# Where the sync queue requests the output weights and the input of tiles 3 to 8 in an attention and mixture-of-experts layer

## The chip, the cores and the metric

The kernel runs on one core of a Trainium2 chip, in one launch. The metric is the device time of an execution in microseconds, and less is better. All times of the trace are counted from the start of the span, which is the time from the first to the last instruction that the profiler recorded.

## The reference, cut to what matters

Two batches of 1024 tokens with 256 features go through two halves of a layer, all in float32. The change touches only the first half, and of that only when its data are fetched.

```
x = x + attention(layernorm(x), ctx)          # 16 heads of 16, 77 keys per batch
    q = layernorm(x) @ w_q.T
    k, v = ctx @ w_k.T, ctx @ w_v.T
    out = softmax(q k^T / 4) v  @ w_o.T
x = x + ffn(layernorm(x))
    shared = silu(x @ sw1.T) * (x @ sw3.T) @ sw2.T
    routed: each token goes to its best 2 of 8 experts, each of the same form as shared
```

## The kernel before, in words

The 2048 tokens are 16 tiles of 128 tokens. The program has one block, with a hand-written list of instructions for each engine (TensorE, VectorE, ScalarE, GpSimd, SyncE), and semaphores between them. Nothing reorders the lists: an instruction that waits holds up all that stand behind it on its engine. The DMA requests are part of these lists too, so a request that waits holds up the requests behind it on the same queue.

The attention half goes through the tiles with a loop over `i` (lines 1143 to 1170 on TensorE). In round `i` TensorE makes the scores of tile `i` (`scores`, lines 986 to 988 by way of `product`), multiplies the probabilities of tile `i - 1` with the values (`attended`, line 1056), transposes the row maxima (`peaks`, line 1031) and subtracts them (`shifted`, line 1039), makes the query of tile `i + 1` (`queries`, line 1010), transposes the probabilities (line 1045), and projects tile `i - 1` with the output weights `wo` (`projected`, line 1072). `queries` waits for its input once per group of tiles: tile 3 waits for `xt2_in`, which stands for the input of tiles 3 to 8 in `x_t`. `projected` waits once, at tile 0, for `wo_in`, and then for `at_out`, ScalarE's copy of the transposed attention (line 474).

Ahead of the loop stands the preparation. TensorE makes the raw keys (line 1130) and the column means of the query's weights (line 1136). VectorE subtracts the means (line 786, semaphore `centred`); TensorE then makes the first query with the centred weights `wq_c`, and after it the raw values (line 999). ScalarE copies the values out of PSUM (`hid`, line 474) and stores them to a scratch tensor `value_rows` in HBM (line 564, 154 KB in rows of 16 floats, semaphore `v_stored`). SyncE reads them back in another layout, with partitions that run over heads and keys (lines 311 and 313, semaphores `v_in0` and `v_in1`, tiles `v_rows` and `act_s`). VectorE spreads the values over three columns of heads (`values`, lines 624 and 626, tile `vals`), and this is what `attended` multiplies with.

The queue of SyncE stands in this order: five requests for the first tiles and the key weights, which wait for nothing (lines 300 to 304); the four reads of the values, which wait for `v_stored`; the input of tiles 3 to 8 (line 315, 768 KB); `wo` (line 316, 256 KB); the residual rows of tiles 3 to 7 (line 317, 640 KB); and then the feed-forward weights in 27 parts of 256 KB by way of four stage buffers `w_stage` (line 323), with the rest of the input (lines 320 and 321) between the fourth and the fifth. ScalarE's queue asks for the context, `wq`, `wv`, the gate and the bias at the start, and stores `value_rows` later. ScalarE and GpSimd split the feed-forward weights into a high and a low part beside the attention (lines 499 and 424), ScalarE from round 2 on.

Behind the attention, tokens are scattered into lists of their experts (GpSimd, line 415), read back by SyncE (line 340) and put through the experts' weights by TensorE (line 992 for the transposes, 986 to 988 for the products).

Of the kernel before, what the change touches and what calls it, by code (L numbers as in the profile page):

```python
# [124 lines left out]
def need(eng, semaphore, value):  # L125
    if value > 0:
        eng.wait_ge(semaphore, value)
# [14 lines left out]
def cols(n, width=DIM):  # L142
    return bass.ds(n * width, width)


def v3(t, a):
    return t.rearrange("p (a b) -> p a b", a=a)


def tiles_of(tokens):  # L150

    return [tokens[b * SEQ:(b + 1) * SEQ, :].rearrange("(p t) d -> p t d", p=P) for b in range(BATCH)]


def rows_of(tokens, t, n):

    u = t % TILES_PER_BATCH
    return tiles_of(tokens)[t // TILES_PER_BATCH][:, u:u + n, :]


def layer_kernel(nc, x, xt, ctxt, wqt, wkt, wvt, wot, gatet, bias, wffn, out):
    def sb(name, n, dt=F32):
        return nc.alloc_sbuf_tensor(name, [P, n], dt)
# [23 lines left out]
    wq_c, wo = (sb(n, KT * DIM) for n in ("wq_c", "wo"))  # L187
# [100 lines left out]


    links_of = [2 + 2 * n + 6 for _, n in GROUPS]  # L290
    links_before = [sum(links_of[:g]) for g in range(len(GROUPS))]

    with nc.Block() as block:

        @block.sync
        def _(sp):
            x_tiles = tiles_of(x)
            resid_tiles = v3(resid[:, :], TILES)
            xt_tiles, turned = xt.rearrange("p (t d) -> p t d", d=DIM), v3(x_t[:, :], TILES)
            sp.dma_start(wk, wkt).then_inc(s["wk_in"], 16)  # L300
            sp.dma_start(turned[:, 0:1, :], xt_tiles[:, 0:1, :]).then_inc(s["xt0_in"], 16)
            sp.dma_start(resid_tiles[:, 0:1, :], x_tiles[0][:, 0:1, :]).then_inc(s["x0_in"], 16)
            sp.dma_start(turned[:, 1:3, :], xt_tiles[:, 1:3, :]).then_inc(s["xt1_in"], 16)
            sp.dma_start(resid_tiles[:, 1:3, :], x_tiles[0][:, 1:3, :]).then_inc(s["x1_in"], 16)


            sp.wait_ge(s["v_stored"], 16)
            sp.wait_ge(s["filled"], 16)
            for b in range(BATCH):
                to = v3(v_rows[b], CHUNKS)  # L310
                sp.dma_start(to[:, 0:WHOLE_CHUNKS, :], value_rows[b, 0:WHOLE_CHUNKS * P, :]
                             .rearrange("(c p) d -> p c d", p=P)).then_inc(s[f"v_in{b}"], 16)
                sp.dma_start(to[0:CHUNK_REST, WHOLE_CHUNKS, :],
                             value_rows[b, WHOLE_CHUNKS * P:, :]).then_inc(s[f"v_in{b}"], 16)
            sp.dma_start(turned[:, 3:9, :], xt_tiles[:, 3:9, :]).then_inc(s["xt2_in"], 16)
            sp.dma_start(wo[:, :], wot).then_inc(s["wo_in"], 16)
            sp.dma_start(resid_tiles[:, 3:TILES_PER_BATCH, :], x_tiles[0][:, 3:, :]).then_inc(s["x2_in"], 16)
            for n, part in enumerate(PART_ORDER):
                if n == STAGES:
                    sp.dma_start(turned[:, 9:, :], xt_tiles[:, 9:, :]).then_inc(s["xt3_in"], 16)  # L320
                    sp.dma_start(resid_tiles[:, TILES_PER_BATCH:, :], x_tiles[1]).then_inc(s["x3_in"], 16)
                need(sp, s["split_lo"], (n - STAGES + 1) * (PART // PIECE))
                sp.dma_start(w_stage[:, cols(n % STAGES, PART)],
                             wffn[:, cols(part, PART)]).then_inc(w_in[n % STAGES], 16)

            sp.wait_ge(s["pads_done"], 4)
            sp.dma_start(lists[EXPERTS * REGION:, :], pad_rows[:, :]).then_inc(s["pad_out"], 16)
            sp.wait_ge(s["counted"], 1)
            _, n_rows = nc.values_load_multi_w_load_instructions(counts_i[0:1, :], engines=(mybir.EngineType.SP,))
            for e in range(EXPERTS):  # L330
                sp.dma_start(lists[bass.ds(n_rows[e] + e * REGION, P), :], pad_rows[:, :]).then_inc(s["pad_out"], 16)
            sp.wait_ge(s["table_step"], TABLE_LINKS)
            sp.wait_ge(s["pad_out"], 16 * (EXPERTS + 1))
            for n in range(ROW_BUFS):
                sp.wait_ge(scat[n], 16 * TOPK * (TILES // ROW_BUFS))
            for j in range(TILES_B):
                row = sp.value_load(row_i[j:j + 1, 0:1], min_val=0, max_val=EXPERTS * REGION)
                need(sp, s["b_t_ps"], j - LIST_BUFS + 1)
                need(sp, s["b_meta"], j - LIST_BUFS + 1)
                sp.dma_start(list_rows[:, cols(j % LIST_BUFS, ROW)],  # L340
                             lists[bass.ds(row, P), :]).then_inc(b_in[j % LIST_BUFS], 16)

            for par in range(2):
                sp.wait_ge(b_out[par], 16 * ((TILES_B + 1 - par) // 2))
            token_rows = results[0:RESULTS, :].rearrange("(t k) d -> t (k d)", k=TOPK)
            for n, (t, tiles) in enumerate(READS):
                sp.dma_start(sum_tiles[:, t:t + tiles, :], rows_of(token_rows, t, tiles)).then_inc(c_in[n], 16)
            for n, (t, tiles) in enumerate(SUM_GROUPS):
                sp.wait_ge(s["c_sum"], n + 1)
                sp.dma_start(rows_of(out, t, tiles), resid_tiles[:, t:t + tiles, :]).then_inc(s["c_out"], 16)  # L350
            sp.wait_ge(s["c_out"], 16 * len(READS))
# [965 lines left out]
```

## Time and profile before

| | us |
|---|---|
| median of 3 runs | 299.66 |
| lowest and highest | 298.84, 300.81 |
| the profiled execution's own time | 295.51 |
| its span | 293.7 |
| TensorE busy in the span | 278.0 (95%) |
| VectorE, ScalarE, GpSimd busy | 185.9, 165.6, 143.8 |

The profiled execution's time holds the span and 1.8 us around it. The trace is one execution, so waits and durations read from it belong to 295.51 us and not to the median.

### The profile page before, as it was taken

To read this page: it belongs to the slowest core of one execution; us is meant where nothing else is said; L and a number is where in the kernel's file an instruction comes from. 1 tells how busy PE (TensorE), PEld (TensorE's weight loads), DVE (VectorE), ACT (ScalarE), POOL (GpSimd) and SP (SyncE) were. 2 spreads that over 40 slices of the span, in tenths; PEclk is the share of its full clock that TensorE was granted. 3 is DMA by queue.
4 is the path that set the end of the run, shared out by engine and by line. 5 is a ranking of instruction groups with operands and counts; after the bars stand their busy time and mean duration, and the time that the engine had idled before them with its cause. 6 is when DMAs were issued, how large, how long until landed. Compare 5 with 4: busy or idle time off the path is not lost.

```text
span 293.7 us, 6561 instructions
## 1 busy us (share of the span) xinstructions
PE 278.0 (95%) x1989; PEld 244.7 (83%) x1989; DVE 185.9 (63%) x700; ACT 165.6 (56%) x404; POOL 143.8 (49%) x234
## 2 busy tenths in 40 slices
PE   7689999999999999999985999999999999999966
PEld 7478889988988999987764898888888998888855
DVE  1648555556765778776874466666766666653675
ACT  2147787778867655556432355665666555554421
POOL 8004776666698837765660013333333333333390
PEclk9999999999999999999998699999999999999999
DMA  7269633343341112211282213333333333211796
GB/s 234 26 158 405 224 102 105 107 108 95 95 138 56 37 39 74 75 55 59 73 234 63 72 54 112 108 98 106 111 110 107 98 107 111 90 44 49 261 390 226
DMA packets 23996, 35.37 MB, mean 120 GB/s; under 512 B 8123, under 2 KB 14907, under 8 KB 23835
## 3 DMA queue, kind: packets, MB, share of 16 engines
q1 hardware_dynamic: 17072, 24.43, 27.1%
q0 software_dynamic: 3408, 9.41, 9.1%
q10 hardware_dynamic: 3483, 1.11, 1.6%
q8 instruction: 18, 0.29, 0.4%
q14 instruction: 15, 0.12, 0.1%
HBM read 22.07 MB, written 12.87 MB: 119 GB/s over the span
## 4 chain that ended last, share of the span: by engine, by line
PE 86%; DMA 4%; DVE 3%; POOL 2%; issue 2%; ACT 1%; SPq 0%; DVEq 0%; POOLq 0%
PE psum L986 15%; PE psum L987 13%; PE psum L988 13%; PE psum L1056 13%; PE psum L992 9%; PE psum L1010 6%; PE psum L1045 5%; PE psum L1072 5%; POOL lists L415 2%; PE psum L1039 2%; DMA lists<-rows,dest 2%; PE psum L1090 1%; DMA value_rows<-hid 1%; PE psum L1125 1%; DMA v_rows<-value_rows 1%
## 5 line engine op out<-in xcount | busy, mean ns | idle before, releaser
L451 POOL DMA_INDIRECT results<-probs_t,place x39 | 37.2, 955 | 81.0 <-ACT probs_t L558 81.0
L1056 PEld LDWEIGHTS psum<-vals,probs_t 128*128 128x128 f32 x320 | 37.9, 192 | 3.2 <-issue 2.6
L1056 PE MATMUL psum<-vals,probs_t 128*128 128x51 f32 x320 | 39.9, 274 | 0.3 <-DVE vals L626 0.3
L424 POOL TENSOR_TENSOR w_lo<-w_stage,w_hi 128x256 fp32r<-128x256 f32 x54 | 37.8, 730 | 4.5 <-ACT w_hi L499 4.5
L415 POOL DMA_INDIRECT lists<-rows,dest x32 | 31.7, 990 | 16.5 <-DVE dest L761 9.3
L543 ACT ACTIVATE act_s<-psum,share 128x256 f32<-128x256 f32 x39 | 18.5, 475 | 32.3 <-PE psum L988 32.3
L986 PE MATMUL psum<-w_lo,x_hi 128*128 (+1 forms) x82 | 36.2, 441 | 0.0
L800 DVE TENSOR_REDUCE row_max<-psum 128x16 f32<-128x1232 f32 x16 | 23.0, 1438 | 20.5 <-PE psum L988 20.4
L854 DVE TENSOR_TENSOR h_lo<-psum,h_hi 128x256 fp32r<-128x256 f32 x55 | 23.3, 423 | 20.1 <-ACT h_hi L474 20.1
L986 PE MATMUL psum<-w_lo,h_hi 128*128 (+1 forms) x110 | 31.8, 289 | 3.3 <-DVE h_lo L854 3.3
L988 PE MATMUL psum<-w_hi,x_hi 128*128 (+1 forms) x82 | 32.4, 395 | 0.0
L987 PE MATMUL psum<-w_hi,x_lo 128*128 (+1 forms) x82 | 32.3, 394 | 0.0
L987 PE MATMUL psum<-w_hi,h_lo 128*128 (+1 forms) x110 | 31.4, 285 | 0.0
L988 PE MATMUL psum<-w_hi,h_hi 128*128 (+1 forms) x110 | 31.3, 284 | 0.0
L850 DVE SCALAR_TENSOR_TENSOR hid<-psum,share,act_s 128x256 f32<-128x256 f32 x39 | 18.9, 484 | 14.8 <-ACT act_s L543 14.8
L986 PEld LDWEIGHTS psum<-w_lo,h_hi 128*128 128x128 f32 x110 | 21.0, 191 | 7.6 <-DVE h_lo L854 4.6
L474 ACT ACTIVATE h_hi<-psum 128x256 fp32r<-128x256 f32 x55 | 20.8, 378 | 10.4 <-PE psum L992 10.4
L488 ACT ACTIVATE probs<-psum,rstd 128x616 f32<-128x616 f32 x32 | 23.0, 770 | 4.7 <-PE psum L1039 4.7
L399 POOL TENSOR_TENSOR rstd<-ve,minus_half 128x1 f32<-128x1 f32 x16 | 9.0, 560 | 30.8 <-DVE ve L649 30.8
L558 ACT ACTIVATE probs_t<-psum,share 128x256 f32<-128x256 f32 x39 | 18.5, 474 | 9.2 <-PE psum L988 8.6
L1045 PE MATMUL psum<-ident,probs 128*128 128x128 f32 x160 | 23.3, 276 | 0.3 <-ACT probs L488 0.3
L987 PEld LDWEIGHTS psum<-w_hi,h_lo 128*128 128x128 f32 x110 | 21.1, 191 | 2.1
(169 smaller groups left out, 677.1 us busy)
## 6 DMA issues: line engine op xcount, KB each, us to landing
w_stage<-in_ffn SPq DMA_DIRECT2D x27, 256.0 KB, 2.8
probs<-lists SPq DMA_DIRECT2D x39, 131.0 KB, 2.1
w_hi<-results SPq DMA_DIRECT2D x7, 512.0 KB, 6.7
out_x<-resid SPq DMA_DIRECT2D x7, 256.0 KB, 2.9
lists<-pad_rows SPq DMA_DIRECT2D x9, 131.0 KB
resid<-in_x SPq DMA_DIRECT2D x1, 1024.0 KB, 10.2
x_t<-in_xt SPq DMA_DIRECT2D x1, 896.0 KB, 8.4
x_t<-in_xt SPq DMA_DIRECT2D x1, 768.0 KB, 5.4
```

Of the source, the lines that this page charges most:

```text
L415: pool.indirect_dma_start(lists, bass.IndirectOffsetOnAxis(ap=dest[:, n:n + 1], axis=0), rows[:, cols(slot, ROW)], None).then_inc(scat[slo ...
L424: pool.tensor_tensor(w_lo[:, to], w_stage[:, of], w_hi[:, to].bitcast(F32), ALU.subtract).then_inc(s["split_lo"], 1)
L451: pool.indirect_dma_start(results, bass.IndirectOffsetOnAxis(ap=place[:, j:j + 1], axis=0), y_rows[:, cols(par)], None).then_inc(b_out[par ...
L488: act.activation(v3(probs[:, cols(g, HALF_COLS)], 2), v3(psum[:, 2 * g * BANK:2 * (g + 1) * BANK], 2)[:, :, 0:BANK_COLS], ACT.Exp, scale=r ...
L800: dve.tensor_reduce(v3(row_max[:, :], 4)[:, :, 0:HEADS_PER_BANK], score_view, axis=AXX, op=ALU.max).then_inc(s["maxed"], 1)
L854: tt(h_lo[:, :], ht_b[:, 0:DIM], h_hi[:, :].bitcast(F32), ALU.subtract).then_inc(s["b_h_low"], 1)
L986: mm(to, ah, bl, start=start, stop=False, skip_group_check=not group)
L987: mm(to, al, bh, start=False, stop=False, skip_group_check=not group)
L988: return mm(to, ah, bh, start=False, stop=stop and group, skip_group_check=not group)
L992: last = pe.transpose(to[:, cols(kt, P)], source[:, cols(kt, P)], ident[:, :])
L1045: last = pe.transpose(bank[TURNED_BANK[c // 4]][:, cols(c % 4, P)], probs[:, cols(c, P)], ident[:, :])
L1056: last = mm(o_b[:, head_base(c) * HV:(head_base(c) + VHEADS) * HV], probs_t[:, cols(c, P)], vals[:, cols(batch * CHUNKS + c, VHEADS * HV)] ...
```

## The change

Two requests of SyncE's queue move. The one for `wo` and the one for the input of tiles 3 to 8 stood behind the four reads of the values. Now they stand ahead of them, in the opposite order between themselves, and wait for `centred`, the semaphore that VectorE raises once the query's weights are centred. Nothing is added but that wait, and nothing is removed.

```
             sp.dma_start(resid_tiles[:, 1:3, :], x_tiles[0][:, 1:3, :]).then_inc(s["x1_in"], 16)
+            sp.wait_ge(s["centred"], 1)
+            sp.dma_start(wo[:, :], wot).then_inc(s["wo_in"], 16)
+            sp.dma_start(turned[:, 3:9, :], xt_tiles[:, 3:9, :]).then_inc(s["xt2_in"], 16)
             sp.wait_ge(s["v_stored"], 16)
             sp.wait_ge(s["filled"], 16)
             for b in range(BATCH):
...
                 sp.dma_start(to[0:CHUNK_REST, WHOLE_CHUNKS, :],
                              value_rows[b, WHOLE_CHUNKS * P:, :]).then_inc(s[f"v_in{b}"], 16)
-            sp.dma_start(turned[:, 3:9, :], xt_tiles[:, 3:9, :]).then_inc(s["xt2_in"], 16)
-            sp.dma_start(wo[:, :], wot).then_inc(s["wo_in"], 16)
             sp.dma_start(resid_tiles[:, 3:TILES_PER_BATCH, :], x_tiles[0][:, 3:, :]).then_inc(s["x2_in"], 16)
```

On SyncE's queue, from the last of the opening requests on, the kernel before has this order. `x_t` is the transposed input, `resid` the rows of the residual, `v_rows` and `act_s` take the values of batch 0 and 1.

```order
L304 DMA resid<-in_x 128x512
L311 DMA v_rows<-value_rows 128x9x16 [waits filled,v_stored]
L313 DMA v_rows<-value_rows 80x16
L311 DMA act_s<-value_rows 128x9x16
L313 DMA act_s<-value_rows 80x16
L315 DMA x_t<-in_xt 128x1536
L316 DMA wo<-in_wo 128x512
L317 DMA resid<-in_x 128x1280
L323 DMA w_stage<-in_ffn 128x512 x4
L320 DMA x_t<-in_xt 128x1792
```

The changed kernel has this order at the same place, with its own line numbers.

```order
L304 DMA resid<-in_x 128x512
L308 DMA wo<-in_wo 128x512 [waits centred]
L309 DMA x_t<-in_xt 128x1536
L316 DMA v_rows<-value_rows 128x9x16 [waits filled,v_stored]
L318 DMA v_rows<-value_rows 80x16
L316 DMA act_s<-value_rows 128x9x16
L318 DMA act_s<-value_rows 80x16
L320 DMA resid<-in_x 128x1280
L326 DMA w_stage<-in_ffn 128x512 x4
L323 DMA x_t<-in_xt 128x1792
```

Two rows moved up past four. The four reads, and all that follows, keep their order. The lists of TensorE, VectorE, ScalarE and GpSimd are the same in both kernels.

## Rows read from the trace of the kernel before

**Rows 1.** The page's chain that ended last: shares of the span by engine.
```profile
PE 86%; DMA 4%; DVE 3%; POOL 2%; issue 2%; ACT 1%; SPq 0%; DVEq 0%; POOLq 0%
```

**Rows 2.** Waits of PE, whole span: total us, times, longest us.
```profile
PE psum L992 <- DMA probs<-lists: 3.2, 1, 3.2
...
PE psum L1056 <- DVE vals L626: 0.3, 1, 0.3
```

**Rows 3.** The chain, 10 to 30 us: start, us, what.
```profile
11.41 3.99 DMA value_rows<-hid
...
15.84 2.09 DMA v_rows<-value_rows
...
18.02 0.80 DVE vals L624 x3
...
18.98 1.99 PE psum L1056 x16
...
24.29 1.00 PE psum L1072 x4
```

**Rows 4.** Timeline, 7 to 30 us: start, us, engine, line, operation [idle before].
```profile
7.12 0.69 DVE L786 TENSOR_TENSOR wq_c<-attn_both,psum 128x512 f32<-128x512 f32 x1
...
17.59 0.43 SPq L315 DMA_DIRECT2D x_t<-in_xt  x1
...
18.06 0.43 SPq L316 DMA_DIRECT2D wo<-in_wo  x1
...
18.54 0.43 SPq L317 DMA_DIRECT2D resid<-in_x  x1
...
23.66 0.38 ACT L474 ACTIVATE attn_both<-psum 128x256 f32<-128x256 f32 x1
...
26.05 0.63 ACT L499 ACTIVATE w_hi<-w_stage 128x512 fp32r<-128x512 f32 x1 [0.75 <-DMA w_stage<-in_ffn]
...
28.49 0.28 ACT L474 ACTIVATE peak_t<-psum 128x128 fp32r<-128x128 f32 x1 [1.14 <-PE psum L1031]
...
29.16 1.16 PE L1010 MATMUL psum<-x_t,wq_c 128*128 128x128 f32 x8
```

**Rows 5.** DMA requests: count, KB each, median us from issue to landing.
```profile
x_t<-in_xt SPq DMA_DIRECT2D x1, 896.0 KB, 8.4
x_t<-in_xt SPq DMA_DIRECT2D x1, 768.0 KB, 5.4
...
wo<-in_wo SPq DMA_DIRECT2D x1, 256.0 KB, 5.6
```

**Rows 6.** Windows at the start: engines' busy us, PEclk, then DMA share and GB/s.
```profile
2.00:3.00 1.00, 1.00 (x7) 1.00 (x6) 0.00 (x0) 0.00 (x0) 0.81 (x6) 1.00 0.70 203
3.00:4.00 1.00, 1.00 (x7) 1.00 (x7) 0.52 (x2) 0.82 (x1) 0.85 (x6) 1.00 1.01 360
...
8.00:12.00 4.00, 3.81 (x28) 2.76 (x28) 2.60 (x9) 0.98 (x2) 0.57 (x1) 1.00 0.00 0
...
12.00:12.25 0.25, 0.00 (x0) 0.00 (x0) 0.25 (x1) 0.00 (x0) 0.00 (x0) 1.00 0.00 0
12.25:12.50 0.25, 0.00 (x0) 0.00 (x0) 0.25 (x1) 0.00 (x0) 0.00 (x0) 1.00 0.66 63
...
27.00:29.00 2.00, 2.00 (x21) 1.89 (x20) 1.93 (x4) 0.86 (x3) 2.00 (x4) 1.00 1.02 427
```

**Rows 7.** Windows at the start of the experts; the number after the brackets is PEclk.
```profile
158.00:160.00 2.00, 0.00 (x0) 0.00 (x0) 0.00 (x0) 0.00 (x0) 0.00 (x0) 0.79 0.28 67
...
164.00:166.00 2.00, 2.00 (x10) 1.90 (x10) 1.14 (x4) 0.75 (x2) 0.00 (x0) 0.50 0.10 28
166.00:168.00 2.00, 2.00 (x14) 1.78 (x13) 1.03 (x7) 0.50 (x2) 0.00 (x0) 1.00 0.00 0
```

**Rows 8.** Timeline of PE around 160 us: start, us, engine, line, operation [idle before].
```profile
156.64 0.38 PE L992 MATMUL psum<-ident,hid 128*128 128x128 f32 x2
160.25 0.66 PE L992 MATMUL psum<-ident,probs 128*128 128x128 f32 x2 [3.23 <-DMA probs<-lists]
```

More of the change, by code:

```diff
@@ L304, in _ @@
             sp.dma_start(resid_tiles[:, 1:3, :], x_tiles[0][:, 1:3, :]).then_inc(s["x1_in"], 16)
+            sp.wait_ge(s["centred"], 1)
+            sp.dma_start(wo[:, :], wot).then_inc(s["wo_in"], 16)
+            sp.dma_start(turned[:, 3:9, :], xt_tiles[:, 3:9, :]).then_inc(s["xt2_in"], 16)
             sp.wait_ge(s["v_stored"], 16)
@@ L314, in _ @@
                              value_rows[b, WHOLE_CHUNKS * P:, :]).then_inc(s[f"v_in{b}"], 16)
-            sp.dma_start(turned[:, 3:9, :], xt_tiles[:, 3:9, :]).then_inc(s["xt2_in"], 16)
-            sp.dma_start(wo[:, :], wot).then_inc(s["wo_in"], 16)
             sp.dma_start(resid_tiles[:, 3:TILES_PER_BATCH, :], x_tiles[0][:, 3:, :]).then_inc(s["x2_in"], 16)
```

## The prediction

> **What bounds the kernel now.** I read the chain that ended last first, because it says whose time is whose. TensorE holds 86% of it and DMA 4% [rows 1], so a transfer matters only where TensorE stands still for it. The waits of TensorE come next. Of all of them two have to do with data from memory: 3.2 us once for the first list of an expert's rows, and 0.3 us once for the masked values [rows 2]. None names `wo` (line 1072) or the input tiles (line 1010). The second wait ends a path in the chain at the start: store of the values at 11.41 for 3.99 us, read back at 15.84 for 2.09 us, masking on VectorE at 18.02, and the first product with them at 18.98 [rows 3]. This path has no slack at all. A microsecond more in the store is a microsecond more for TensorE, and since TensorE is never idle by choice afterwards, for the end. Had the path been shorter, only 0.3 us could have been won, because TensorE was still busy with the scores of tile 1 until 0.3 us before.
>
> **The two transfers, as they were.** The trace has no wait for them, but how near were they?
>
> `wo` was requested at 18.06 [rows 4] and landed 5.6 us later [rows 5], so at 23.7. Its first reader, line 1072, also waits for ScalarE's copy of the transposed attention, which starts at 23.66 and takes 0.38 us [rows 4], so ends at 24.04. It started at 24.29, behind the transposes of TensorE's own list [rows 3]. So `wo` was 0.4 us early against the copy and 0.6 us early against TensorE. Fetching it earlier wins 0.
>
> The input of tiles 3 to 8 was requested at 17.59 [rows 4] and took 5.4 us [rows 5]: there at 23.0. Its first reader is the query of tile 3 at 29.16 [rows 4], 6.2 us later. Fetching it earlier wins 0.
>
> **What is late next.** With both gone from behind the reads, the residual rows and the weight stages are requested two issues earlier: 18.54 less 17.59 is 0.95 us [rows 4], and 1024 KB less lies ahead of the stages in the queue. 1024 KB are 1.049 MB, at the 427 GB/s of 27 to 29 us [rows 6] 2.5 us. ScalarE waited 0.75 us for the first stage, at 26.05 [rows 4]. That wait goes. But ScalarE then stands still for 1.14 us ahead of the next row maxima at 28.49, until TensorE has them [rows 4]. So the 0.75 us turn into more of that idle time: 0 on the path. GpSimd's low parts start earlier by as much, and nobody on the path waits for them in this stage. Sum of the gains on the path: 0.
>
> **What the two transfers meet at their new place.** The semaphore `centred` is raised at 7.12 + 0.69 = 7.81 [rows 4]. SyncE's two issues of 0.43 us each follow, at about 7.9 and 8.3. Behind the new wait stand the four reads of the values. They wait for the store until 15.4 in any case, so the added wait and the added 0.9 us of issue cost them nothing: SyncE is free again at 8.8, 6.6 us ahead of them. Their own request starts at the same moment after the store's landing.
>
> The DMA engines moved nothing from 8 to 12 us [rows 6]. The store was issued at 11.41 [rows 3] and its data moved from 12.25 on: 0 GB/s in the quarter before, 63 in that one [rows 6]. So data follow their issue by about 0.85 us, and the data of `wo` start at about 8.7. How long do 1.049 MB take? The trace has loads in HBM-to-SBUF form at three rates [rows 6]: 427 GB/s with the queue full gives 2.5 us, 360 GB/s in the first burst gives 2.9 us, and the slowest full microsecond, 203 GB/s while that burst built up, gives 5.2 us. They end at 11.2, 11.6 or 13.9. I take 360 GB/s, since the first burst is the nearest case: an idle system, a few requests of like size. Then the transfers end 0.65 us before the store's data start at 12.25, and the store does not notice. Cost 0, with bounds of 0 and 13.9 less 12.25, that is 1.7 us, if the store had to stand behind the whole of the rest.
>
> The store and the two loads are issued from different queues. The Trainium skill, page "DMA: Bandwidth & Descriptors", section "Issuing engines are not separate DMA queues", says that DMAs from the scalar and the sync engine all run on the same 16 engines and interleave. The trace before cannot show it for this pair, since the two never overlapped there. By that rule an overlap is paid in the store, and with the overlap of the slow case above the sum would be up to 1.7 us slower; with no overlap it says nothing against the change. Without the rule the sum is the same 0.
>
> **Sum.** The profiled execution of 295.51 us (span 293.7 and 1.8 around it) would stay at 295.5. The runs' median is 4.15 us above it. I have no row for these 4.15 us, so I carry them over unchanged: 299.66 + 0 is 299.6 to 299.7. I predict 299.6.
>
> **The rivals.**
>
> *A. `wo` is late in the usual execution.* Its margin was only 0.4 us, and the runs are 4.15 us longer than the profiled one. If in those `wo` took as long as the slowest like transfer behind a full queue, the 8.4 us of the 896 KB request [rows 5], it would land at 26.5 against 24.04: 2.4 us of standing still, which the change removes, since at the new place it lands some 10 us ahead of its reader. The time is then 297.2. Against it: that request had the four stages ahead of it and more bytes, and `wo` had only 768 KB before it. The input tiles cannot add to it; with 8.4 us they land at 26.0, still ahead of 29.16. Chance 0.12.
>
> *B. The store is held up: slower.* The place is the store of `value_rows` in 12.25 to about 14.3 us. It decides whether the two loads still have data to move at 12.25, that is, whether they run at under 1.049 MB in 3.55 us, 295 GB/s. Each microsecond of overlap costs at most one. The price is up to 1.7 us, so up to 301.3; I would expect 0.7 where it happens, 300.3. For it: the microsecond at 203 GB/s. Against it: the next one at 360. Chance 0.12.
>
> *C. The clock's dip at the experts' start changes.* TensorE ends a transpose at 157.0 and starts the next at 160.25, after 3.23 us for the first list [rows 8]. The granted clock was 0.79 on average in 158 to 160, 0.50 in 164 to 166, and 1.00 from 166 on [rows 7]: the level of 1.2 GHz in place of 2.4 GHz, from some point in the wait until about 166. Work from 160.25 to 166, 5.75 us, went at half speed, which cost about 2.9 us. A shift in where the work stands could remove the dip (296.8) or double it (302.5). Nothing in the change acts on that wait, which hangs on GpSimd's scatters and their landing, so I give this 0.10, half to each side.
>
> *D. It does not do what it says:* the requests leave at the new place but something else in the queue keeps them, and they land where they did. The time is 299.7. SyncE's list before them is empty from 3.1 us on, so I give it 0.02.
>
> The forecast itself, both transfers early and nobody waiting for either, has 0.64.
>
> **How the numbers follow.** About 1% is what a measurement of this kernel can tell from no change, and that is 3.0 us here. The forecast, D, B and most of A lie inside it. Faster by over 1% takes the good half of C (0.05), the far end of A together with the scatter of the runs (0.04): 0.09. Slower by over 1% takes the bad half of C (0.05) and B at its bound with the scatter of the runs (0.03): 0.08. The rest, 0.83, is within 1%. The range goes from A's 297.2 to B's 301.3, which leaves out C and the tails: 297.2 to 301.4.
>
> **What would show it.** In the changed profile: (1) issues of `wo` and `x_t` at about 7.9 and 8.3 us; (2) DMA moving 250 to 430 GB/s somewhere in 8.7 to 12 us, where it was 0; (3) the store's row in the chain at 3.9 to 4.1 us, as before, and TensorE's first product with the values within 0.2 us of 18.98. If the store's row reads 4.5 us or more, B is right. (4) ScalarE's wait of 0.75 us for the first stage gone, and its idle time ahead of the third row maxima grown by about as much. (5) Line 1072 still starting right behind line 1045, at about 24.3. The prediction is wrong if runs come out below 297 with the start of the trace unchanged up to 25 us; then the gain would lie in executions that the profile did not catch (A), or later, at the dip of the clock (C).

## The result and the profile after

| | before | changed |
|---|---|---|
| median of 20 runs each, us | 299.35 | 303.68 |
| lowest and highest | 294.56, 304.23 | 297.75, 307.10 |
| profiled execution, its span | 295.51, 293.7 | 301.95, 300.2 |

The ratio is 1.013, with a 95% interval of 1.0085 to 1.0175; this ratio and those of the experiments leave out runs of either kernel that lie over 1.5% above its fastest (8 of 20 stay for the changed kernel here, and 4 of 12 in the first experiment), while the medians hold all. The changed kernel is slower by about 1.3%. I had forecast 299.6 and no difference.

The two transfers did what the change says. The requests on SyncE's queue in the changed kernel's timeline (start, us, engine, line, operation):

```profile
7.35 0.33 SPq L308 DMA_DIRECT2D wo<-in_wo  x1
...
7.72 0.43 SPq L309 DMA_DIRECT2D x_t<-in_xt  x1
...
10.93 0.55 ACTq L567 DMA_DIRECT2D value_rows<-hid  x1
...
14.94 0.39 SPq L316 DMA_DIRECT2D v_rows<-value_rows  x1
```

Its DMA requests (count, KB, us to landing), to be set against [rows 5]:

```profile
x_t<-in_xt SPq DMA_DIRECT2D x1, 768.0 KB, 4.5
...
wo<-in_wo SPq DMA_DIRECT2D x1, 256.0 KB, 2.7
```

And its windows at the start (busy us of the engines, PEclk, DMA share, GB/s), to be set against [rows 6]:

```profile
9.00:10.00 1.00, 1.00 (x6) 0.59 (x4) 0.93 (x3) 0.00 (x0) 0.00 (x0) 1.00 1.12 397
10.00:11.00 1.00, 1.00 (x13) 0.81 (x12) 0.15 (x1) 0.60 (x1) 0.57 (x1) 1.00 0.95 399
11.00:12.00 1.00, 0.31 (x6) 0.05 (x2) 0.64 (x1) 0.00 (x0) 0.00 (x0) 1.00 0.51 162
12.00:13.00 1.00, 0.05 (x1) 0.08 (x1) 1.00 (x2) 0.00 (x0) 0.00 (x0) 1.00 0.83 80
```

The loads reached nearly 400 GB/s in the gap where nothing had moved before. With the slower quarters at both ends, their data moved from about 8.25 to 11.75, so 1.049 MB took some 3.5 us, 300 GB/s on average (an estimate from finer windows of the same trace). The store's data began right behind them, in the quarter from 11.75 on. The store was issued at 10.93 and read back from 14.94 on, so it had landed within 4.01 us, against 3.99 in the kernel before [rows 3]. The store did not notice the loads, and `wo` landed at 10.0, 14 us ahead of its reader. The whole start ran 0.5 us earlier in this execution: the raw keys, which wait for the first transfers, were done sooner.

The loss that the change brings is at tile 2. The changed kernel's timeline from 25 to 30 us, on ScalarE, VectorE, GpSimd and TensorE:

```profile
25.19 1.17 ACT L502 ACTIVATE w_hi<-w_stage 128x512 fp32r<-128x512 f32 x2
...
25.88 1.85 DVE L627 TENSOR_TENSOR vals<-act_s,val_mask 128x160 f32<-128x160 f32 x3
25.92 3.07 POOL L427 TENSOR_TENSOR w_lo<-w_stage,w_hi 128x256 fp32r<-128x256 f32 x4 [0.72 <-ACT w_hi L502]
...
27.65 0.71 DVE L629 COPY vals<-val_mask 128x30 f32<-128x30 f32 x1
28.26 1.43 DVE L803 TENSOR_REDUCE row_max<-psum 128x16 f32<-128x1232 f32 x1
...
29.75 0.33 PE L1034 MATMUL psum<-ident,row_max 128*128 128x128 f32 x1 [1.44 <-DVE row_max L803]
```

The same stretch of the kernel before, where its low part (line 424) came later:

```profile
25.85 0.78 DVE L624 TENSOR_TENSOR vals<-act_s,val_mask 128x160 f32<-128x160 f32 x3
...
26.55 0.18 DVE L626 COPY vals<-val_mask 128x30 f32<-128x30 f32 x1
...
26.64 1.43 DVE L800 TENSOR_REDUCE row_max<-psum 128x16 f32<-128x1232 f32 x1
...
26.76 2.79 POOL L424 TENSOR_TENSOR w_lo<-w_stage,w_hi 128x256 fp32r<-128x256 f32 x4 [1.60 <-ACT w_hi L499]
...
28.12 0.33 PE L1031 MATMUL psum<-ident,row_max 128*128 128x128 f32 x1
```

Read the second and fourth rows of the first fence against the first two of the second. VectorE masks the values of batch 1 in both at about 25.9. In the kernel before it takes 0.78 us and the copy 0.18. In the changed kernel GpSimd's first low part starts 0.04 us after the masking, and then the masking takes 1.85 and the copy 0.71. The row maxima start 1.6 us later, and TensorE, which had not waited there, stands still for 1.44 us. Before, GpSimd came 0.03 us after VectorE was through. The stage that it works on lands earlier in the changed kernel, because two requests no longer stand ahead of it.

The three maskings one by one, first of the kernel before and then of the changed kernel (shortest, median and longest in ns):

```profile
L624 DVE TENSOR_TENSOR vals<-act_s,val_mask x3: 312/313/314, 25.8 to 26.3; 128x160 f32<-128x160 f32 x3
...
L627 DVE TENSOR_TENSOR vals<-act_s,val_mask x3: 320/842/851, 25.9 to 26.9; 128x160 f32<-128x160 f32 x3
```

One of the three kept its 0.32 us, and two took 0.53 and 0.54 more. The copy took 0.53 more. These three add up to the 1.60 us.

The starts of the 16 row maxima, changed less before, are -0.50 us at tile 0, +0.30 at tile 1, +1.62 at tile 2, and 1.60 to 1.67 up to tile 13. So from tile 2 on nothing more is lost for some 85 us. Of the way from -0.50 to +1.62, only the last 1.32 us are the meeting. The 0.80 us between tiles 0 and 1 go with a granted clock of 0.50, the level of 1.2 GHz, that this execution had from 15 to 18 us and the profiled execution of before had not (PE busy, PEclk, DMA share, GB/s; before, then changed):

```profile
15.00:18.00 3.00, 2.44 (x22) 1.00 0.35 36
...
15.00:18.00 3.00, 2.65 (x14) 0.50 0.49 50
```

Both kernels have a wait of TensorE of 1.6 us ahead of that, at tile 0. After tile 13 the difference grows to 2.47 at tile 14, 2.97 at tile 15 and 6.5 at the end of the span. Those later steps are looked at in the part on the prediction.

### The profile page after: what moved, and what is told of

It is laid out like the page before. It is cut to its first block, busy times and chain, and to the rows that moved or that the text cites. A ratio compares the mean times of both kernels' runs of the same rounds, so it can differ in the third digit from the quotient of the medians.

```text
span 300.2 us, 6561 instructions
## 1 busy us (share of the span) xinstructions
PE 281.8 (94%) x1989; PEld 247.7 (82%) x1989; DVE 187.6 (62%) x700; ACT 165.5 (55%) x404; POOL 144.4 (48%) x234
## 4 chain that ended last, share of the span: by engine, by line
PE 88%; DVE 5%; ACT 3%; another core or an unknown queue 2%; issue 1%; POOL 0%; DVEq 0%; POOLq 0%
PE psum L989 16%; PE psum L991 15%; PE psum L990 14%; PE psum L1059 11%; PE psum L995 9%; PE psum L1048 5%; PE psum L1013 5%; PE psum L1075 4%; PE psum L1042 2%; PE psum L1093 2%; ACT probs L491 1%; PE psum L1128 1%; DVE row_max L803 1%; PE psum L1034 1%
## 5 line engine op out<-in xcount | busy, mean ns | idle before, releaser
L1048 PE MATMUL psum<-ident,probs 128*128 128x128 f32 x160 | 24.2, 285 | 0.5 <-ACT probs L491 0.3
```

Source lines behind the costliest of these rows:

```text
L1048: last = pe.transpose(bank[TURNED_BANK[c // 4]][:, cols(c % 4, P)], probs[:, cols(c, P)], ident[:, :])
```

## The experiments

Each execution has a mean granted clock on record, except those of the kernel before in the first comparison. Within each kernel the time went down as the clock went up: one line through the executions of the changed kernel, the experiments and the kernel before beside them, with one slope for all and a level for each, gives 2.46 us for 0.01 of clock. "At equal clock" below is each kernel's mean, moved along that line to a clock of 0.98 (standard error 0.2 to 0.4 us, 0.7 for the tenth). The line says how the two go together, and not that all of it is the clock's doing. An execution of 360 us of the kernel before at clock 0.73 is left out of it and of the mean clock. The kernel before differed between occasions, so each group has its own.

| occasion | kernel | runs | median us | mean clock | us at equal clock | ratio to before (95%) |
|---|---|---|---|---|---|---|
| first | before | 20 | 299.35 | not on record | | |
| first | changed | 20 | 303.68 | 0.969 | 300.5 | 1.013 (1.009 to 1.018) |
| 2 | before | 29 | 300.13 | 0.976 | 299.0 | |
| 2 | 1: low part waits | 12 | 299.97 | 0.978 | 299.0 | 0.991 (0.985 to 0.998) |
| 2 | 2: stage first | 12 | 301.21 | 0.977 | 300.6 | 1.000 (0.994 to 1.006) |
| 2 | 3: `wo` alone | 12 | 302.63 | 0.973 | 300.5 | 1.006 (0.999 to 1.012) |
| 2 | 4: `x_t` alone | 6 | 304.11 | 0.968 | 300.8 | 1.018 (1.011 to 1.025) |
| 3 | before | 23 | 297.31 | 0.981 | 297.7 | |
| 3 | 5: wait filled | 12 | 297.45 | 0.982 | 298.7 | 1.003 (0.999 to 1.006) |
| 3 | 6: low part waits, filled | 6 | 296.93 | 0.983 | 297.9 | 0.989 (0.982 to 0.996) |
| 3 | 7: before, filled | 14 | 294.83 | 0.988 | 297.5 | 0.988 (0.984 to 0.992) |
| 4 | before | 23 | 300.89 | 0.976 | 299.3 | |
| 4 | 8: changed | 12 | 304.32 | 0.969 | 301.0 | 1.005 (0.996 to 1.014) |
| 4 | 9: as 5 | 12 | 299.75 | 0.984 | 300.7 | 1.001 (0.995 to 1.007) |
| 4 | 10: as 6 | 6 | 302.86 | 0.974 | 302.4 | 1.011 (1.000 to 1.021) |
| 5 | before | 23 | 299.85 | 0.977 | 299.3 | |
| 5 | 11: as 7 | 12 | 302.05 | 0.982 | 302.2 | 1.007 (1.002 to 1.011) |
| 5 | 12: as 6 | 12 | 301.99 | 0.979 | 301.9 | 1.007 (1.003 to 1.012) |

**1. The changed kernel, with GpSimd's first low part held back.**

```
 def low_part(n):
+    if n == 0:
+        pool.wait_ge(s["v_done"], 2 * (VHEADS + 1))
     pool.wait_ge(s["split_hi"], n + 1)
```

> The changed kernel, but GpSimd's first low part (line 427, round 2) waits until VectorE has written all values (v_done at 8). Theory P (the change brings the first weight stage forward, so GpSimd's low parts run beside VectorE's masking of the values of batch 1, both read two SBUF operands, the masking takes 2.56 us instead of 0.96, and TensorE waits 1.4 us for the row maxima of tile 2): the three maskings of batch 1 are back at 0.27 us each and the copy at 0.2, TensorE has no wait of over 0.3 us for row maxima at tile 2, and the time is 1.3 to 1.6 us under the changed kernel's, so it stands at about 1.01 of the kernel before if the clock dips make up the rest, or 1.00 if they were a consequence. Rival S (the DMA traffic itself slows VectorE's reads): the maskings stay slow, since the traffic of 25 to 28 us is the same, and the time stays 4 us over the kernel before.

The timeline of this kernel at the same place:

```profile
26.69 0.79 DVE L629 TENSOR_TENSOR vals<-act_s,val_mask 128x160 f32<-128x160 f32 x3
27.39 0.18 DVE L631 COPY vals<-val_mask 128x30 f32<-128x30 f32 x1
27.48 1.43 DVE L805 TENSOR_REDUCE row_max<-psum 128x16 f32<-128x1232 f32 x1
27.65 2.78 POOL L429 TENSOR_TENSOR w_lo<-w_stage,w_hi 128x256 fp32r<-128x256 f32 x4 [1.65 <-DVE vals L631]
...
28.96 0.33 PE L1036 MATMUL psum<-ident,row_max 128*128 128x128 f32 x1
```

GpSimd stands still for 1.65 us, and VectorE is back at 0.79 and 0.18. TensorE's row has no wait. Both transfers are still at their new place, with much the same traffic beside the masking: 396 to 443 GB/s in the single microseconds from 25 to 28, against 408 to 459 in the changed kernel. The median is that of the kernel before, and so is the time at equal clock. The ratio of 0.991 would make it 0.9% faster, but only four of its runs carry that, and the means of all runs, 0.4 us apart with a standard error of 0.8, do not bear it out. So the moved requests cost nothing that can be seen but this meeting, and they gain nothing either. The rival by which the traffic itself slows VectorE is out.

**2. The kernel before, with one stage asked for earlier.** Nothing of the change is in it.

```
 sp.dma_start(wo[:, :], wot).then_inc(s["wo_in"], 16)
+sp.dma_start(w_stage[:, cols(0, PART)], wffn[:, cols(PART_ORDER[0], PART)]).then_inc(w_in[0], 16)
 sp.dma_start(resid_tiles[:, 3:TILES_PER_BATCH, :], ...)
 for n, part in enumerate(PART_ORDER):
...
+    if n == 0:
+        continue
```

> The kernel before, with one request moved: the first weight stage is asked for ahead of the residual rows of tiles 3 to 7. Nothing of the change is in it; only that stage lands about 1.5 us earlier. Theory P: ScalarE splits it at 25.3 instead of 26.05, GpSimd's first low part starts at about 25.9 on VectorE's masking, the masking and copy take 2.3 to 2.6 us, TensorE waits 1.2 to 1.5 us for the row maxima of tile 2, and the time is 1.3 us or more over the kernel before. Rival S, or a rival by which the loads beside the store of the values cost the time: nothing changes in the masking, and the time is within 0.5 us of the kernel before.

Its timeline:

```profile
25.86 1.86 DVE L627 TENSOR_TENSOR vals<-act_s,val_mask 128x160 f32<-128x160 f32 x3
25.91 3.07 POOL L427 TENSOR_TENSOR w_lo<-w_stage,w_hi 128x256 fp32r<-128x256 f32 x4 [0.72 <-ACT w_hi L502]
...
27.64 0.71 DVE L629 COPY vals<-val_mask 128x30 f32<-128x30 f32 x1
...
29.74 0.33 PE L1034 MATMUL psum<-ident,row_max 128*128 128x128 f32 x1 [1.47 <-DVE row_max L803]
```

These are the changed kernel's numbers without the change. At equal clock it is 1.6 us slower than the kernel before. The median is 1.1 us higher, where I had expected 1.3 or more, and the ratio of 1.000 shows no difference, so the price rests on the figure at equal clock and on the wait of 1.47 us in the trace.

**3 and 4. One of the two requests alone.** In each, one line moves as in the change and the other stays.

> Only the request for wo moves to its new place, the input of tiles 3 to 8 stays. Theory P: the stages are behind 256 KB less and one issue less, so the first lands 0.5 to 0.7 us earlier, ScalarE starts at about 25.3 to 25.5, GpSimd's first low part at 26.0 to 26.2 still meets the last masking and the copy, and TensorE waits 0.5 to 1.4 us at tile 2; the time is between the two kernels. Rival by which the bulk of 768 KB beside the store is what costs: like the kernel before within 0.5 us.

> Only the request for the input of tiles 3 to 8 moves, wo stays behind the reads. Theory P: the first stage lands over 1 us earlier, so the full collision as in the changed kernel: masking and copy of batch 1 at 2.4 to 2.6 us, a wait of TensorE of about 1.4 us at tile 2, and the time of the changed kernel within 1 us. Rival by which wo's landing matters: like the kernel before.

Timeline of the kernel with `wo` alone moved:

```profile
25.86 1.32 DVE L625 TENSOR_TENSOR vals<-act_s,val_mask 128x160 f32<-128x160 f32 x3
26.10 3.02 POOL L425 TENSOR_TENSOR w_lo<-w_stage,w_hi 128x256 fp32r<-128x256 f32 x4 [0.92 <-ACT w_hi L500]
27.10 0.71 DVE L627 COPY vals<-val_mask 128x30 f32<-128x30 f32 x1
...
29.20 0.43 PE L1032 MATMUL psum<-ident,row_max 128*128 128x128 f32 x1 [0.92 <-DVE row_max L801]
```

And with `x_t` alone:

```profile
26.37 1.85 DVE L625 TENSOR_TENSOR vals<-act_s,val_mask 128x160 f32<-128x160 f32 x3
26.42 3.07 POOL L425 TENSOR_TENSOR w_lo<-w_stage,w_hi 128x256 fp32r<-128x256 f32 x4 [0.73 <-ACT w_hi L500]
28.15 0.71 DVE L627 COPY vals<-val_mask 128x30 f32<-128x30 f32 x1
...
30.25 0.33 PE L1032 MATMUL psum<-ident,row_max 128*128 128x128 f32 x1 [1.46 <-DVE row_max L801]
```

The meeting is dosed by GpSimd's start. 0.24 us after VectorE's, the masking takes 1.32 us and TensorE waits 0.92; 0.05 us after it, 1.85 and 1.46. The three maskings of the kernel with `wo` alone, one by one, show how:

```profile
L625 DVE TENSOR_TENSOR vals<-act_s,val_mask x3: 319/320/848, 25.9 to 26.3; 128x160 f32<-128x160 f32 x3
```

Here two of them kept their 0.32 us and one took 0.53 more, and so did the copy. So the dose comes in steps of one VectorE instruction: each that came after GpSimd's start paid 0.53 us. Either request alone brings it on. At equal clock both kernels are 1.5 and 1.8 us over the kernel before. For `wo` alone that is more than its wait of 0.92 in the one profiled execution, its ratio of 1.006 (0.999 to 1.012) does not resolve it, and the rest is not explained.

**5, 8 and 9. The changed kernel with TensorE's wait of round 2 filled, and as it is.** The filling is six matmuls whose results nobody uses; the profile counts each as two.

```
+for _ in range({2: 6}.get(i, 0)):
+    mm(r_b[:, 0:P], mean_of[:, :], mean_of[:, :])
 peaks(i)
```

> The changed kernel with six matmuls of 128x128 into an unused bank ahead of the row maxima's transpose of round 2, where TensorE stands still for 1.4 us in the changed kernel; their results are not used. Theory P with clock: the masking is as slow as in the changed kernel, and line of the row maxima starts at the same 29.7 us or at most 0.2 us later, so at equal granted clock the time is the changed kernel's; but the granted clock no longer falls between 30 and 36 us, the mean clock over the runs is 0.975 or more instead of 0.969, and the median is 301.5 to 302.5 instead of 303.7. Rival (the lower clock of the changed kernel has another cause than this wait, or was chance): mean clock and median stay as in the changed kernel, within 0.5 us.

> The changed kernel as it is, for a comparison with its own variants on one chip, since the kernel before had a median of 300.1 us beside the first four experiments and 297.3 beside the next three. Theory P with clock: a mean clock of 0.970 or less where the kernel before has 0.976 to 0.981, a median 3.5 to 4.5 us over the kernel before, of which 1.5 us remain at equal clock. Rival (the first comparison's excess over 1.5 us was chance): a median 1 to 2 us over the kernel before with the same mean clock.

> The changed kernel with six unused matmuls in TensorE's wait of round 2, beside the changed kernel itself. Theory P with clock: 1.5 to 3 us under the changed kernel's median and a mean clock higher by 0.006 to 0.012, while the masking stays slow and the time at equal clock is the same within 0.5 us. Rival: no difference between the two.

Timeline of the ninth run's kernel: the meeting is as before, but TensorE works through it.

```profile
25.88 1.85 DVE L627 TENSOR_TENSOR vals<-act_s,val_mask 128x160 f32<-128x160 f32 x3
...
28.15 1.57 PE L1154 MATMUL psum<-mean_of 128*128 128x128 f32 x12
...
29.76 0.33 PE L1034 MATMUL psum<-ident,row_max 128*128 128x128 f32 x1
```

What the filling can save is seen in the windows of the fourth run's kernel, which waits there unfilled (the number behind the brackets is PEclk):

```profile
27.00:30.00 3.00, 1.79 (x16) 1.66 (x15) 3.00 (x4) 0.00 (x0) 2.49 (x4) 1.00 0.99 395
30.00:33.00 3.00, 2.75 (x15) 2.39 (x16) 2.26 (x9) 1.98 (x4) 0.74 (x2) 0.59 0.60 221
33.00:36.00 3.00, 3.00 (x16) 3.00 (x16) 0.67 (x3) 1.55 (x5) 0.99 (x2) 0.50 0.01 3
```

and of the ninth's:

```profile
30.00:33.00 3.00, 3.00 (x28) 2.71 (x28) 2.12 (x10) 2.85 (x7) 0.74 (x2) 1.00 0.33 95
```

TensorE was busy for 1.79 of 3 us in the unfilled one, and then the granted clock fell to the level of 1.2 GHz. In 33 to 36 us it did 16 matmuls, where the ninth run's kernel at a full clock did 28 in 30 to 33. Such a fall at 30 to 36 us stands in the profiles of runs 2, 3 and 4, all with the wait. It stands in none of the kernel before, run 1, or the filled ones. It does not come each time: the profiles of the changed kernel, the first and the eighth run's, have the wait and a full clock there.

The eighth run repeats the first comparison. Its median is 3.4 us over the kernel before's, a little less than the 3.5 to 4.5 that I had expected, and so is its mean (standard error 1.0). Its ratio of 1.005 (0.996 to 1.014), which three of its runs carry, does not resolve the difference by itself.

On that occasion the filled kernel had a median 4.6 us under the changed one's. The mean is 4.0 us lower (standard error 1.1), and the mean clock higher by 0.015 (0.969 and 0.984, standard error 0.0045), with which 3.6 us go by the line above. At equal clock they differ by 0.4 us, within error, as expected, since the meeting is untouched; the filled one is still 1.4 us over the kernel before. I had expected a drop of 1.5 to 3 us, so the size was off. The filled kernel's clock was also above the 0.976 of the kernel before, so the filling did more than take the new wait away. On occasion 3 the filled kernel had a median 0.1 us over the kernel before's, 1.0 more at equal clock, and the same mean clock within error. The changed kernel was not run beside it there, so the fifth run does not show what its filling did.

**6, 7, 10, 11 and 12. Filling the waits that both kernels have.** Six such matmuls in round 0 and twelve ahead of the first rows of the experts, in the kernel of run 1 and in the kernel before.

```
+for _ in range({0: 6}.get(i, 0)):
+    mm(r_b[:, 0:P], mean_of[:, :], mean_of[:, :])
 peaks(i)
...
 if n + 3 == EARLY:
     pe.wait_ge(s["split_lo"], PARTS * (PART // PIECE))
+    pe.wait_ge(s["x1_done"], TILES)
+    for _ in range(12):
+        mm(a_b[:, 0:P], mean_of[:, :], mean_of[:, :])
     rows_transposed(n + 3 - EARLY)
```

> The first experiment's kernel (GpSimd's first low part waits for the values) with six unused matmuls in TensorE's wait of 1.6 us in round 0 and twelve in its wait of 3.2 us for the first rows of the experts. If waits of TensorE are what lets the granted clock fall, the dips near 15 and 157 us go, the mean clock rises to 0.985 or more, and the median is 297 to 298.5, under both kernels. Rival (the dips come whatever TensorE does): clock 0.976, median 300 to 300.5.

> The kernel before with the same unused matmuls in round 0 and ahead of the experts. Same expectation as for the kernel with the waiting low part, since that wait does nothing without the earlier stage: clock 0.985 or more and a median of 297 to 298.5, within 0.7 us of it. If the moved requests gained anything beside the collision, this one is slower than that by the gain.

> The changed kernel with GpSimd's first low part held back and unused matmuls in round 0 and ahead of the experts, again, since six runs were few. At equal clock like the kernel before; mean clock 0.985 or more; median 2 to 3 us under the kernel before and 5 to 7 us under the changed kernel.

> The kernel before with six unused matmuls in round 0 and twelve ahead of the experts, on another occasion, since the variant with the same matmuls on the changed kernel was faster than the kernel before once and slower once. If the matmuls keep the clock up: mean clock higher than the kernel before by 0.005 or more and a median 1.5 to 3 us under it. Rival (the first gain was the luck of the runs): within 1 us of it.

> The changed kernel with the waiting low part and the same unused matmuls, a third time. If the collision was all that the moved requests cost, it lies within 1 us of the kernel before with these matmuls. Rival (holding GpSimd back or the moved requests cost time elsewhere): 2 us or more over it at equal clock.

On occasion 3 they looked like a gain of 1.1 and 1.2%. On the next two they were a loss of 0.7 to 1.1%, where I had expected gains of 1.5 to 3 us. Occasions 3 and 5 were on the same chip, so another chip is not the reason. So no filled version beats the kernel before on each occasion that it ran on, and the first gain has to be put down to the occasion. The mean clock did rise in both runs of the filled kernel before, by 0.007 and 0.005, but on occasion 5 it paid 3 us at equal clock. The profile of run 11 shows one reason: TensorE waited elsewhere, where nothing was filled.

```profile
157.70 0.58 PE L986 MATMUL psum<-w_lo,h_hi 128*128 128x256 f32 x1 [2.69 <-issue]
```

Those 2.7 us had come before the twelve matmuls. These took 2.84 us from 166.22 on, with the list's rows already there, so they stood behind a wait instead of in one. In the profile of run 7 they started at 161.27, and 0.16 us of the wait for the list was left behind them. The 2.84 us are near the 3 us lost at equal clock. That this holds for the other executions of occasion 5 was not shown.

Filling does not keep the clock up by itself either. Run 7's profile, with round 0 filled, has this at 21 to 24 us, and the same clock at 24 to 27 (busy us of the engines, PEclk, DMA share, GB/s):

```profile
21.00:24.00 3.00, 3.00 (x17) 2.63 (x16) 0.56 (x3) 0.30 (x2) 0.00 (x0) 0.50 0.96 369
```

TensorE's longest idle time between 12 and 21 us was 0.56 us there, and the clock fell all the same, to the level of 1.2 GHz.

What the pairs with the same matmuls do tell is a second check of run 1. The kernel with the moved requests and the held low part is at 301.99 and the kernel before at 302.05 (runs 12 and 11), and at equal clock they are 297.9 and 297.5 on occasion 3 (runs 6 and 7).

## Why the prediction was wrong

The forecast of 299.6 in 297.2 to 301.4 missed 303.68.

- *"Fetching it earlier wins 0"*, for both transfers: right. Run 1 keeps both fetches and equals the kernel before. Rival A, `wo` late in the usual execution, is thereby out.
- *The store is not held up*: right, but with luck. 4.01 us against 3.99. I had taken 360 GB/s for the whole transfer and 0.65 us to spare. The loads reached 397 and 399 GB/s, but only between slow ends, and took about 3.5 us, 300 GB/s on average, hardly more than the 295 below which rival B begins. They were through just as the store's data started. Rival B did not happen, and the interleaving of the two queues was never tried, since they still did not overlap.
- *TensorE's first product with the values within 0.2 us of 18.98*: 19.00, which is chance. The start ran 0.5 us earlier, and TensorE lost that again at the granted clock of 0.50 from 15 to 18 us. The values were there before it, so the path that I had said to have no slack was not the last one in this execution.
- *ScalarE's 0.75 us go*: right, it starts at 25.19 without a wait.
- *"GpSimd's low parts start earlier by as much, and nobody on the path waits for them in this stage. Sum of the gains on the path: 0."* This step failed. Nobody waits for them, that is true, but they run beside somebody. I asked what waits for GpSimd, not what it shares. They started 0.84 us earlier and met the masking of VectorE, which TensorE waits for. What the runs showed in its place is 1.60 us more for the masking and the copy (2.56 against 0.96), 1.44 us of it as a wait of TensorE, and 1.5 to 1.8 us at equal clock (1.7 for the changed kernel, 1.5 to 1.8 for runs 2 to 4). The clue stood in the trace: GpSimd had started 0.03 us after the copy was over.
- *Rival C, the clock*: I had given the bad half 0.05 and tied it to the wait at 157 us. The changed kernel's clock was 0.969 on both occasions, against 0.976 for the kernel before beside the second, and that difference, two standard errors, is 1.6 us by the line. So on occasion 4 the mean difference of 3.4 us is 1.7 at equal clock and 1.6 that go with the clock. That the new wait at 28 us lowers the clock is likely and not shown. For it: with the wait filled, the mean clock rises to 0.984. Against it: that is above the kernel before too, and run 2 has the same wait, a fall of the clock behind it in its profile, and a mean clock like the kernel before's. Run 1 speaks for the meeting as the root of both halves: without it, the time and the mean clock (0.978) are those of the kernel before beside it (0.976). By what path the meeting costs the second half stays open.
- *"I have no row for these 4.15 us, so I carry them over unchanged."* The profiled execution was one with a clock of 0.988 and without the standstills below, and ordinary ones are not. Carrying them over was harmless for the median of before. It may have hidden that a new wait is dearer in ordinary executions than its own length.

The Trainium skill has the rule that I should have weighed. The page "SBUF — State Buffer", section "Who interferes with whom", says that a VectorE instruction with two inputs in SBUF contends with a GpSimd instruction that reads SBUF, since its second input comes by the read interface that the two share. It also says that the order of issue decides who blocks. The trace agrees: the maskings read `act_s` and `val_mask`, the one that started 0.04 us ahead of GpSimd kept its 0.32 us, and the two behind it took 0.84 and 0.85. The page also says that `tensor_reduce` never contends and that an instruction with at most one SBUF input does not, outside certain modes. The row maxima beside the same low parts took 1.43 us in both kernels. By the page the copy can contend too, and it went from 0.18 to 0.71. No run exchanges the operands, so the shared interface as the reason is the page's and not shown here; that GpSimd's work beside it slows the masking is shown by runs 1 and 2.

**What the clock and the standstills do to the rest.** The profiled executions differ by 6.5 us. 1.6 is there at tile 2. Two more steps are standstills of ScalarE that end without a releaser that I can name. For the first of them the row names TensorE's transposes, but these were done at 117.72, 0.98 us before it ends. The changed kernel's rows on ScalarE and TensorE:

```profile
118.70 0.38 ACT L477 ACTIVATE attn_both<-psum 128x256 f32<-128x256 f32 x1 [1.28 <-PE psum L995]
...
159.00 0.39 ACT L477 ACTIVATE h_hi<-psum 128x256 fp32r<-128x256 f32 x1 [5.33 <-remote]
...
159.89 0.58 PE L989 MATMUL psum<-w_lo,h_hi 128*128 128x256 f32 x1 [4.51 <-DVE h_lo L857]
```

The same two in the kernel of run 11, in which no request is moved:

```profile
117.77 0.38 ACT L474 ACTIVATE attn_both<-psum 128x256 f32<-128x256 f32 x1 [1.32 <-PE psum L992]
...
156.80 0.38 ACT L474 ACTIVATE h_hi<-psum 128x256 fp32r<-128x256 f32 x1 [3.64 <-remote]
```

The other way round, the profile of run 5 has the moved requests and neither standstill. So they are not the change's. The long one is absent in the profiled executions of the kernel before and of runs 5, 6 and 7, the last three of them all on occasion 3, and it is present, at 2.2 to 5.6 us, in the others. What they are stays open. It also stays open how much of the lower mean clock comes by way of the later places where TensorE waits.

## What to carry to other kernels

When a request moves up, everything behind it on its queue lands earlier too: follow those landings to the engine that starts on them, and ask beside whom it then works, not only who waits for it. VectorE instructions with two operands in SBUF that TensorE waits for want GpSimd's SBUF work kept off them, and a wait in front of GpSimd's first instruction does that for free where GpSimd has time, as in run 1. A wait of TensorE can cost more than its length, since the clock may fall behind it. Compare kernels over many executions and with their clocks, and take a single profile's total for one draw.

## What the runs showed of the hardware that I had not expected

- Three maskings of 128x160 elements with two SBUF operands went from 0.78 us together to 1.85 beside GpSimd subtractions from SBUF, a copy of 128x30 from 0.18 to 0.71. Each instruction that started after GpSimd's first lost 0.53 us, and the one that started 0.04 us before it lost nothing. Meanwhile, a reduction from PSUM beside the same subtractions stayed at 1.43. GpSimd lost less: four pieces in 3.07 us against 2.79.
- 1.05 MB in two requests reached 397 and 399 GB/s in the two full microseconds of an otherwise idle stretch, took about 3.5 us in all (300 GB/s, an estimate from quarters of a microsecond), and did not disturb a store whose data started right behind them.
- The granted clock fell to 0.50 for 6 us in run 7's profile although TensorE had not been idle for more than 0.56 us at a time in the 9 us before.
- The executions of the kernel before spread over 294.6 to 304.2 us in the first comparison, and where the clock of each is listed, the time goes with it, at 2.46 us for 0.01 of mean granted clock.
